# A causal attention kernel: twelve probability buffers, and weighted sums issued five steps behind the scores instead of three

## The chip, the cores and the metric

The program runs on one core of a Trainium2 chip. A core has a matrix engine (TensorE, PE), a vector engine (VectorE, DVE), a scalar engine (ScalarE, ACT), a general engine (GpSimd, POOL), and a queue engine (SyncE, SP) that issues transfers and here computes nothing. Each engine runs its own list of instructions in order and waits on semaphores that others raise. The metric is the device time of one execution in microseconds (us), lower is better.

## The reference

A block with layer norm, then attention and a ternary feed-forward side by side, both added to the input. The change touches the attention alone: 4 batches, 16 heads of 16 dimensions, 2048 positions, causal.

```
xn = layernorm(x)                                   # x: (4, 2048, 256)
q, k, v = heads of xn (two small projections each, rotary part on half of q and k)
scores = (q @ k.T) / sqrt(16);  masked above the diagonal
y = softmax(scores) @ v;  out = x + y @ Wc + ffn(xn)
```

## The kernel before

Three stages follow each other: projections and feed-forward (to about 520 us), attention (to about 1925 us), and the output projection. `attention` works through 16 *quads*, a quad being four heads of one batch. One quad has two kinds of work, and they run at the same time, for different quads.

**Maxima.** For softmax each query row needs its maximum first. `SEQ` lists 139 *entries* for a quad: PE writes a block of scores (128 queries by up to 512 keys) into one of three banks `sm` (L1146), and DVE reduces it to one number a row (L1109; L1094 where the diagonal's mask is added; L1105 where `excess` is added, which stands for a second block: PE forms the difference of two blocks in `st`, L1155 and L1158, and ACT takes its positive part, L1044). Three entries of the list, the *rows*, gather the maxima of a group of queries: DVE reduces them (L1070), PE transposes them (L1142), DVE splits them into two fp16 parts `mh` and `ml` (L1078, L1080), and SP copies these with 16 small transfers into spare rows of `Q` in SBUF (`load_m`, L939). There they act as an additive term of the scores. The groups are the query chunks (0, 1), (2) and (3), a chunk being 512 queries.

**Probabilities.** For a chunk `c` the key blocks `j` are taken in turn, each as a *pair* of *units* of two heads. A quad has 40 pairs: 4 in chunk 0, then 8, 12 and 16. PE computes a unit's scores into one of the two buffers `st` (`scores`, L1170), ACT writes the exponential to one of eight buffers `prob` (L1051), POOL clears the triangle of diagonal blocks (L1009), and PE adds the pair's weighted sums and row sums into the bank `pv` (`weighted_sums`, L1183). Within a chunk the last four pairs are diagonal, 512, 384, 256 and 128 columns wide. After a chunk's last sums ACT copies `pv` to `Y` (`evac`, L1034), and the next chunk's first sums wait for that copy (`pv_read`).

**The order.** PE's order in one quad is the string `TIMETABLE`, a letter for each step: `m` an entry of the maxima (75 entries, `AHEAD`, are always done for the quad before its scores begin, so the string begins with entry 75 of this quad and ends with entry 74 of the next), `x` a difference, `s` a unit of scores, `w` the weighted sums of a pair. ACT follows the same string for `x`, `s` and the copies. `LAG` says with how many pairs of the quad before the string's `w` begin: with 3 the first three `w` are pairs 37 to 39 of the quad before. DVE's order is that of the entries alone.

**SP's order for a quad** (`body` in `@block.sync`) is fixed in the code: wait until all sums of the quad before are done (`pair_used`), load Q and K of the quad after next (12 transfers, L859), load V of the next one (L928), then `load_m` for group 1 and group 2 of this quad and group 0 of the next, then wait for the copy of chunk 3 (`pv_read`), and store `Y` and its row sums (8 transfers, L956 and L957). The copy of chunk 3 stands in the next quad's string, behind that string's `LAG`-th `w`. The first unit of chunk 2 (unit 24) waits on PE until the rows of group 1 have landed (`m_loaded`), the first unit of chunk 3 (unit 48) for those of group 2. In the last quad nothing is loaded, and in the first nothing is stored first.

Of the kernel before, what the change touches and what calls it, by code (L numbers as in the profile page):

```python
# [733 lines left out]

ST, SM, PT = 2, 3, 8
SLOTS = 3
UNITS = sum(2 * G * (c + 1) for c in range(TC))
PAIRS = UNITS // 2  # L740
# [41 lines left out]

AHEAD = 75
XAHEAD = sum(e < AHEAD + LEAD for e in EXCESS)
LAG = 3

ORDER = [(c, j, CH - P * max(0, j - SUB * c)) for c in range(TC) for j in range(SUB * (c + 1))]

# [1 line left out]
def block_width(t, k):  # L790
# [4 lines left out]


TIMETABLE = (
    "ssmmwmmsmswsmmswxmmxmwsmsmmssmwmswsmsmmwxmmsmwmmsmmxmwmmssmmwmmsmsws"
    "mmxmxmmwmmssmmsmsssmmwmsmxmmsmwsmmwxmsmmwsmmmsmswsmmsmwsmsmmwsmmxmms"
    "mmwsmsmmwmsmmswmsmmswsmxmmswmsmsmsmmwsmmmsmwwmmssmmwsmmmswsmmmswsmmm"  # L800
    "swmmssmwsmmmswsmmswsmmmswmsmsmmwsmmsmwmsmsmmwmsmxmmsmwmmsxmmsmwsmsm"
)


def tokens():

    plan, e, x, u, n = [], AHEAD, XAHEAD, 0, -LAG
    for c in TIMETABLE:
# [9 lines left out]
        else:  # L818
            plan.append(("sums", -1 if n < 0 else 0, n % PAIRS))
            n += 1  # L820
    assert (e, x, u, n) == (NE + AHEAD, NX + XAHEAD, 2 * PAIRS, PAIRS - LAG)
    return plan
# [39 lines left out]
def attention(nc, w, scr):  # L862

    with ExitStack() as ctx:
# [52 lines left out]
        def quads(body):  # L917

            for quad in range(NQ):
                body(quad, quad % SLOTS, quad == NQ - 1)  # L920
# [211 lines left out]
        def _(pe):  # L1132
# [41 lines left out]
            def weighted_sums(quad, slot, n, last):  # L1174
                c, j, width = order[n]
                if j == 0:
                    pe.wait_ge(pv_read, quad * TC + c + 1)
                if diag[n]:
                    pe.wait_ge(masked, quad * DIAG + 2 * sum(diag[:n + 1]))
                else:  # L1180
                    pe.wait_ge(exp_done, unit_done(quad, NUMBERS[last][2 * n + 1]))
                for h in range(G):
                    i = pe.matmul(pv[2 * DH * h:2 * DH * (h + 1), CH - width:CH], lhsT=V[slot][:, j, h, :],  # L1183
                                  rhs=prob[(slot * UNITS + 2 * n + h // 2) % PT][:, h % 2, 0:width],
                                  start=j == 0, stop=j == SUB * (c + 1) - 1, tile_position=(0, 2 * DH * h))
                    if h == G - 1:
                        i.then_inc(pair_used, 1)
# [30 lines left out]
            quads(body)  # L1218
            for n in range(PAIRS - LAG, PAIRS):
                weighted_sums(NQ - 1, (NQ - 1) % SLOTS, n, True)  # L1220
# [220 lines left out]
```

## Time and profile before

| | us |
|---|---|
| median of 3 runs (lowest, highest) | 2054.63 (2052.05, 2055.58) |
| the profiled execution | 2050.78 |
| its span | 2049.0 |
| PE busy | 1939.1 (95%) |
| DVE busy | 1795.2 (88%) |
| ACT busy | 1578.8 (77%) |
| POOL busy | 359.0 (18%) |
| attention, steady quads: one quad | 84.4 to 86.6 |

The engines' busy times are those of the profiled execution. PE's times are modelled, so its share is no measure of how near it is to its peak. The granted clock is given as a share of 2.4 GHz, and 0.50 is 1.2 GHz. ACT does nothing in the output projection, which is why its share of the whole is lower than its share of a quad.

### The profile page before, as it was taken

To read this page: it belongs to the slowest core of one execution; us is meant where nothing else is said; L and a number is where in the kernel's file an instruction comes from. 1 tells how busy PE (TensorE), PEld (TensorE's weight loads), DVE (VectorE), ACT (ScalarE), POOL (GpSimd) and SP (SyncE) were. 2 spreads that over 40 slices of the span, in tenths; PEclk is the share of its full clock that TensorE was granted. 3 is DMA by queue.
4 is the path that set the end of the run, shared out by engine and by line. 5 is a ranking of instruction groups with operands and counts; after the bars stand their busy time and mean duration, and the time that the engine had idled before them with its cause. 6 is when DMAs were issued, how large, how long until landed. Compare 5 with 4: busy or idle time off the path is not lost. (4 is left out here: it accounts for less than half of the span.)

```text
span 2049.0 us, 42600 instructions
## 1 busy us (share of the span) xinstructions
PE 1939.1 (95%) x14289; PEld 733.6 (36%) x14289; DVE 1795.2 (88%) x4744; ACT 1578.8 (77%) x2078; POOL 359.0 (18%) x618
## 2 busy tenths in 40 slices
PE   7899999999699999999999999999999999999698
PEld 6455555555222222222222222222222222222165
DVE  5699999999889999999999989999999999997187
ACT  2566666666089999999899989999999999999500
POOL 0112221111112121221212212122121221211000
PEclk8999999999589999999999999999999999999889
DMA  4133333325411230311303113031130321300376
GB/s 165 42 89 94 99 97 102 86 87 126 91 28 23 32 54 2 54 30 26 54 2 54 31 24 54 2 54 32 24 54 2 53 38 18 54 2 13 101 211 206
DMA packets 146213, 123.32 MB, mean 60 GB/s; under 512 B 82068, under 2 KB 132668, under 8 KB 144572
## 3 DMA queue, kind: packets, MB, share of 16 engines
q1 hardware_dynamic: 137324, 112.55, 25.3%
q10 hardware_dynamic: 8720, 8.65, 1.4%
q8 instruction: 89, 1.46, 0.3%
q14 instruction: 80, 0.66, 0.1%
HBM read 69.50 MB, written 50.86 MB: 59 GB/s over the span
## 5 line engine op out<-in xcount | busy, mean ns | idle before, releaser
L1051 ACT ACTIVATE prob<-st 128x1024 f32<-128x1024 f32 (+3 forms) x1280 | 1071.7, 898 | 83.3 <-PE st L1170 75.4
L1183 PE MATMUL pv<-prob,V 128*32 128x512 f32 (+3 forms) x5120 | 598.6, 542 | 0.1
L1146 PE MATMUL sm<-K,Q 48*128 48x512 f16 (+3 forms) x2176 | 542.1, 350 | 17.0 <-DVE pm L1109 4.7
L1094 DVE CUSTOM_DVE_ANT_0 sm<-sm,mask 128x128 f32<-128x128 f32 (+3 forms) x1024 | 490.5, 510 | 61.1 <-PE sm L1146 53.7
L1109 DVE TENSOR_REDUCE pm<-sm 128x1 f32<-128x512 f32 x768 | 494.6, 685 | 15.0 <-PE sm L1146 12.6
L1170 PE MATMUL st<-Q,K 50*128 50x512 f16 (+3 forms) x2560 | 472.5, 353 | 21.5 <-ACT prob L1051 10.9
L1009 POOL TENSOR_SCALAR_AFFINE_SELECT prob<-prob 128x256 f32<-128x256 f32 x512 | 206.1, 409 | 1116.5 <-ACT prob L1051 1111.4
L1146 PEld LDWEIGHTS sm<-K,Q 48*128 48x128 f16 x2176 | 173.8, 94 | 392.6 <-DVE pm L1109 156.6
L1105 DVE CUSTOM_DVE_ANT_0 sm<-sm,excess 128x512 f32<-128x512 f32 x384 | 264.8, 716 | 25.5 <-PE sm L1146 16.2
L1170 PEld LDWEIGHTS st<-Q,K 50*128 50x128 f16 x2560 | 125.3, 93 | 408.5 <-ACT prob L1051 321.7
L1044 ACT ACTIVATE excess<-st 128x1024 f32<-128x1024 f32 x188 | 190.4, 1032 | 5.1 <-DVE pm L1105 0.7
L1183 PEld LDWEIGHTS pv<-prob,V 128*32 128x32 f32 x5120 | 102.5, 108 | 161.0 <-issue 123.7
L1094 DVE DVE_READ_ACCUMULATOR2_ANT pm<- 128x1 f32 x1024 | 144.5, 141 | 0.2
L639 ACT ACTIVATE g<-bank 128x512 f32<-128x512 f32 x128 | 76.7, 599 | 54.7 <-PE bank L708 54.7
L669 PE MATMUL bank<-wWP,gh 128*128 128x256 f16 x512 | 113.7, 273 | 0.0
L669 PE MATMUL bank<-wWP,gl 128*128 128x256 f16 x512 | 113.5, 272 | 0.0
L533 DVE SCALAR_TENSOR_TENSOR gl<-g,wlnw,gh 128x512 f16<-128x512 f32 x128 | 91.9, 758 | 6.5 <-ACT gh L642 6.5
L1296 DVE RECIPROCAL rl<-sums 16x512 f32<-16x512 f32 x16 | 53.3, 3333 | 47.3 <-DMA sums<-scratch_l 47.3
L642 ACT ACTIVATE gh<-g,wlnw 128x512 f16<-128x512 f32 x128 | 93.5, 731 | 0.0
L1155 PE MATMUL st<-K,Q 48*128 48x512 f16 x384 | 81.0, 389 | 9.1 <-ACT prob L1051 7.2
L644 ACT ACTIVATE g<-g 128x512 f32<-128x512 f32 x128 | 81.4, 636 | 0.0
L1158 PE MATMUL st<-NK,Q 48*128 48x512 f16 x384 | 80.7, 384 | 0.0
(151 smaller groups left out, 1896.2 us busy)
## 6 DMA issues: line engine op xcount, KB each, us to landing
Q<-scratch_q SPq DMA_DIRECT2D x102, 128.0 KB, 4.0
K<-scratch_k SPq DMA_DIRECT2D x102, 128.0 KB, 6.2
x<-in_x SPq DMA_DIRECT2D x18, 512.0 KB, 4.5
scratch_v<-Vs SPq DMA_DIRECT2D x64, 128.0 KB, 2.0
scratch_r<-R SPq DMA_DIRECT2D x16, 512.0 KB, 3.2
V_raw<-scratch_v SPq DMA_DIRECT2D x16, 512.0 KB, 8.8
scratch_y<-Y SPq DMA_DIRECT2D x64, 128.0 KB
Yt<-scratch_y SPq DMA_DIRECT2D x16, 512.0 KB, 5.8
```

The source lines that it names most:

```text
L533: dve.scalar_tensor_tensor(out=gl[:, hc, :], in0=g[:, hc, 0, :], scalar=w["lnw"][:, hc:hc + 1], in1=gh[:, hc, :], op0=ALU.mult, op1=ALU.su ...
L642: act.activation(gh[:, hc - 1, :], g[:, hc - 1, 0, :], ACT.Copy, scale=w["lnw"][:, hc - 1:hc])\
L669: pe.matmul(bank[s][:, 0:C], lhsT=x[:, hc, s * P:(s + 1) * P], rhs=w["WP"][:, hc, :], start=hc + k == 0, stop=hc + k == HC)
L1009: pool.affine_select(out=x, in_=x, compare_op=ALU.is_ge, fill=0.0, base=0, pattern=[[0, 2], [1, P]], channel_multiplier=-1).then_inc(maske ...
L1044: act.activation(excess[((slot + ahead) % SLOTS * NX + k) % EXCESSES][:, :, :], st[number % ST][:, :, :], ACT.Relu)\
L1051: act.activation(prob[(slot * UNITS + k) % PT][:, :, 0:width], st[number % ST][:, :, 0:width], ACT.Exp)\
L1094: dve.tensor_tensor_reduce(x, x, mask[:, CH - width:], 1.0, -3e38, ALU.add, ALU.max, pm[:, row, t, k:k + 1]).then_inc(sm_read, 1)
L1105: dve.tensor_tensor_reduce(x, x, excess[(slot * NX + r) % EXCESSES][:, h % 2, :], 1.0, -3e38, ALU.add, ALU.max, pm[:, row, t, k:k + 1]).th ...
L1109: dve.tensor_reduce(out=pm[:, row, t, k:k + 1], in_=x, axis=AX.X, op=ALU.max).then_inc(sm_read, 1)
L1146: pe.matmul(dst[:, 0:block_width(t, k)], lhsT=Q[slot][r, h // 2, t * P:(t + 1) * P], rhs=K[slot][r, h // 2, k * CH:k * CH + block_width(t, ...
L1170: i = pe.matmul(st[number % ST][:, a, 0:width], lhsT=K[slot][r, u % 2, j * P:(j + 1) * P], rhs=Q[slot][r, u % 2, (c + 1) * CH - width:(c + ...
L1183: i = pe.matmul(pv[2 * DH * h:2 * DH * (h + 1), CH - width:CH], lhsT=V[slot][:, j, h, :], rhs=prob[(slot * UNITS + 2 * n + h // 2) % PT][: ...
```

## The change

`PT`, the number of probability buffers, goes from 8 to 12; a score unit can be computed six pairs ahead of its sums instead of four. `LAG` goes from 3 to 5, so that each string's first five `w` belong to the quad before. The string is another order of the same letters. After the last quad five pairs of sums are left to do instead of three.

```
-ST, SM, PT = 2, 3, 8
+ST, SM, PT = 2, 3, 12
...
-LAG = 3
+LAG = 5
...
-    "ssmmwmmsmswsmmswxmmxmwsmsmmssmwmswsmsmmwxmmsmwmmsmmxmwmmssmmwmmsmsws"
...
+    "mxxmmwmsmmswmsmmswsmmswsmmswssmmwsmmmswsmsmwmmsmsmmwxmxmmwmmsmswmsmm"
```

DVE's order is the same. PE and ACT keep their instructions but for the order. These are ACT's rows from the start of a quad's units to its copy of chunk 3 of the quad before. `prob<-st` is a unit's exponential (128x1024 is two heads of 512 columns), `excess<-st` a difference, `Y<-pv` the copy. Before:

```order
L1051 ACTIVATE prob<-st 128x2x256
L1051 ACTIVATE prob<-st 128x2x128 x2
L1051 ACTIVATE prob<-st 128x1024 x2
L1051 ACTIVATE prob<-st 128x2x384 x2
L1051 ACTIVATE prob<-st 128x2x256 x2
L1034 ACTIVATE Y<-pv 128x512
```

And now:

```order
L1051 ACTIVATE prob<-st 128x2x128 x2
L1044 ACTIVATE excess<-st 128x1024 x2
L1051 ACTIVATE prob<-st 128x1024 x2
L1051 ACTIVATE prob<-st 128x2x384 x2
L1051 ACTIVATE prob<-st 128x2x256 x2
L1051 ACTIVATE prob<-st 128x2x128 x2
L1034 ACTIVATE Y<-pv 128x512
```

The 2x128 rows ahead of the others close the quad before. Behind them the copy came after six units; now it comes after two differences and eight units.

These are ACT's rows from behind that copy to the end of chunk 1; the first unit of chunk 2 follows them. Before:

```order
L1044 ACTIVATE excess<-st 128x1024 x2
L1051 ACTIVATE prob<-st 128x2x128 x2
L1051 ACTIVATE prob<-st 128x1024 x5
L1034 ACTIVATE Y<-pv 128x512
L1044 ACTIVATE excess<-st 128x1024
L1051 ACTIVATE prob<-st 128x1024 x2
L1044 ACTIVATE excess<-st 128x1024
L1051 ACTIVATE prob<-st 128x1024 x3
L1051 ACTIVATE prob<-st 128x2x384 x2
L1044 ACTIVATE excess<-st 128x1024 x2
L1051 ACTIVATE prob<-st 128x2x256 x2
L1051 ACTIVATE prob<-st 128x2x128 x2
```

And now:

```order
L1051 ACTIVATE prob<-st 128x1024 x8
L1034 ACTIVATE Y<-pv 128x512
L1044 ACTIVATE excess<-st 128x1024 x2
L1051 ACTIVATE prob<-st 128x1024 x2
L1051 ACTIVATE prob<-st 128x2x384 x2
L1044 ACTIVATE excess<-st 128x1024 x2
L1051 ACTIVATE prob<-st 128x2x256 x2
L1051 ACTIVATE prob<-st 128x2x128 x2
```

Two differences and two units of 128 columns have gone from between the copy and chunk 2. Counted in the two strings, with all letters:

| stretch of the string | letters before | letters now |
|---|---|---|
| start to the last `w` of the quad before | 7 m, 6 s, 0 x, 3 w | 13 m, 8 s, 2 x, 5 w |
| from there to unit 24 (chunk 2) | 36 m, 18 s, 6 x, 9 w | 29 m, 16 s, 4 x, 7 w |
| the rows entry of group 2 to unit 48 (chunk 3) | 17 m, 10 s, 1 x, 5 w | 14 m, 9 s, 0 x, 4 w |
| fewest units between a pair's own and its sums | 2 | 6 |

## Rows read from the trace of the kernel before

**Rows 1.** Busy time in one quad: us, each engine, granted clock, DMA share, GB/s.

```profile
827.15:911.68 84.53, 82.52 (x671) 23.02 (x668) 78.36 (x235) 79.34 (x97) 16.60 (x35) 1.00 0.21 33
```

**Rows 2.** Waits of the whole run: who waited for whom, us, times, longest.

```profile
PEld pv L1183 <- POOL prob L1009: 13.0, 53, 0.5
...
PEld pv L1183 <- ACT Y L1034: 6.6, 33, 0.4
...
PEld st L1170 <- DMA Q<-ml: 6.4, 12, 1.3
```

**Rows 3.** Timeline of SP in a steady quad: start, duration, instruction, count.

```profile
827.77 0.35 SPq L956 DMA_DIRECT2D scratch_y<-Y  x1
...
830.86 3.48 SPq L859 DMA_DIRECT2D Q<-scratch_q  x6
...
837.66 7.39 SPq L939 DMA_DIRECT2D Q<-mh  x4
845.10 2.42 SPq L939 DMA_DIRECT2D Q<-ml  x4
```

**Rows 4.** Timeline of ACT: the copy of chunk 3 in six quads.

```profile
827.15 0.59 ACT L1034 ACTIVATE Y<-pv 128x512 f32<-128x512 f32 x1
...
911.68 0.59 ACT L1034 ACTIVATE Y<-pv 128x512 f32<-128x512 f32 x1
...
996.34 0.60 ACT L1034 ACTIVATE Y<-pv 128x512 f32<-128x512 f32 x1
...
1082.49 0.60 ACT L1034 ACTIVATE Y<-pv 128x512 f32<-128x512 f32 x1
...
1166.85 0.60 ACT L1034 ACTIVATE Y<-pv 128x512 f32<-128x512 f32 x1
...
1253.45 0.60 ACT L1034 ACTIVATE Y<-pv 128x512 f32<-128x512 f32 x1
```

**Rows 5.** Timeline of PE's weight loads: chunk 2 begins, wait for the rows.

```profile
848.72 0.12 PEld L1170 LDWEIGHTS st<-Q,K 50*128 50x128 f16 x2 [0.28 <-DMA Q<-ml]
...
933.27 0.10 PEld L1170 LDWEIGHTS st<-Q,K 50*128 50x128 f16 x2 [0.30 <-DMA Q<-ml]
...
1018.41 0.11 PEld L1170 LDWEIGHTS st<-Q,K 50*128 50x128 f16 x4 [0.79 <-DMA Q<-ml]
...
1104.06 0.12 PEld L1170 LDWEIGHTS st<-Q,K 50*128 50x128 f16 x2 [0.28 <-DMA Q<-ml]
...
1189.45 0.11 PEld L1170 LDWEIGHTS st<-Q,K 50*128 50x128 f16 x4 [1.33 <-DMA Q<-ml]
```

**Rows 6.** ACT's waits from the copy to chunk 2 of one quad.

```profile
ACT prob L1051 <- PE st L1170: 1.4, 4, 0.5
```

**Rows 7.** Timeline of ACT: units back to back, 512 and 128 columns wide.

```profile
829.62 0.66 ACT L1051 ACTIVATE prob<-st 128x256 f32<-128x256 f32 x2
...
879.36 7.65 ACT L1051 ACTIVATE prob<-st 128x1024 f32<-128x1024 f32 x8
```

**Rows 8.** Timeline of PE: one pair's sums, and what follows them.

```profile
879.70 1.06 PE L1183 MATMUL pv<-prob,V 128*32 128x512 f32 x8
880.70 0.39 PE L1170 MATMUL st<-Q,K 50*128 50x512 f16 x2
```

**Rows 9.** Busy time and granted clock behind two longer waits, as in rows 1.

```profile
1020.00:1022.00 2.00, 2.00 (x16) 0.78 (x10) 1.25 (x6) 1.17 (x2) 0.00 (x0) 0.50 0.00 0
1190.00:1193.00 3.00, 3.00 (x18) 0.81 (x16) 1.51 (x4) 1.89 (x2) 0.00 (x0) 0.50 0.00 0
```

**Rows 10.** Timeline of all engines: from group 2's transposition to unit 48.

```profile
864.68 0.33 PE L1142 MATMUL sm<-ident,m 128*128 128x128 f32 x1
...
868.19 2.47 SPq L939 DMA_DIRECT2D Q<-ml  x4
...
874.67 0.39 PE L1170 MATMUL st<-Q,K 50*128 50x512 f16 x2
```

**Rows 11.** Timeline of PE: the last three pairs of sums of attention.

```profile
1920.62 1.76 PE L1183 MATMUL pv<-prob,V 128*32 128x384 f32 x24
```

More of the change, by code:

```diff
@@ L797 @@
 TIMETABLE = (
-    "ssmmwmmsmswsmmswxmmxmwsmsmmssmwmswsmsmmwxmmsmwmmsmmxmwmmssmmwmmsmsws"
-    "mmxmxmmwmmssmmsmsssmmwmsmxmmsmwsmmwxmsmmwsmmmsmswsmmsmwsmsmmwsmmxmms"
-    "mmwsmsmmwmsmmswmsmmswsmxmmswmsmsmsmmwsmmmsmwwmmssmmwsmmmswsmmmswsmmm"
-    "swmmssmwsmmmswsmmswsmmmswmsmsmmwsmmsmwmsmsmmwmsmxmmsmwmmsxmmsmwsmsm"
+    "mxxmmwmsmmswmsmmswsmmswsmmswssmmwsmmmswsmsmwmmsmsmmwxmxmmwmmsmswmsmm"
+    "smxmxmmwmmssmsmssmsmmwsmsmmwsmmxmwsmmxmwwmmssmwmmsmswsmmmswmssmmwmms"
+    "msmmwsmmmswmmsmswmmssmwsmmssmswmmsmsmmwsmmsmmwwsmmsmwmmsmxmmsmwmsmms"
+    "wmsmmswmmsmswmmsmswmsmswmmsmsmmxmmsmwmsmmswsmmmsmxmmswmsmmxsmmwmsms"
 )
```

## The prediction

> **What bounds the kernel now.** I first read the busy time of the engines in one steady quad, taken from one copy of chunk 3 to the next [rows 1]. In 84.53 us PE is busy for 82.52, ACT for 79.34 and DVE for 78.36, and the clock is full. No engine has more than some 6 us to spare, and with two buffers `st` and three banks `sm` between them none can run far ahead. So 5 or 6 us of a quad are lost in handing over, and whatever stops PE for longer than these few buffers last stops all three.
>
> Next the list of waits [rows 2], for what the change can take away. The sums' weight loads wait for POOL's triangle for 13.0 us in the whole run, 53 times, and for the copy of `pv` for 6.6 us. The same list has a third wait, a small one: scores wait 6.4 us for the transfer of `ml`, 12 times. It is small in sum, but an engine that waits twelve times for a little is one whose supplier is only just in time. So I followed that supplier back in the timelines.
>
> SP's timeline of one quad [rows 3] starts at 827.77, right behind ACT's copy of chunk 3, which began at 827.15 [rows 4]. It stores Y until 830.86, issues the Q, K and V loads, then comes to the rows of group 1 at 837.66. Four tiny transfers of `mh` take it 7.39 us there, which I read as a queue full of the 2 MB before them, and the four of `ml` are out at 845.10 + 2.42 = 847.52. PE's first unit of chunk 2 goes at 848.72, after waiting 0.28 us for them [rows 5], so landing takes 1.2 us. From the copy to that release it is 848.72 - 827.15 = 21.57 us. The four other quads shown [rows 4, 5] have 21.59, 22.07, 21.57 and 22.60; the mean is 21.9. Without the wait PE would have been there after 21.57 - 0.28 = 21.29 us, and in the others after 21.29, 21.28, 21.29 and 21.27. So two chains of nearly equal length start at the copy: SP's, 21.6 to 22.6 us, and the order's, 21.3 us. SP's chain wins by 0.3 to 1.3.
>
> **The change part by part.** *The copy moves, unit 24 does not.* The later `w` put the copy of chunk 3 behind 13 entries and 8 units instead of 7 and 6, while unit 24 stays at the same place in the string (letter 84, from 85). SP's list is unchanged and hangs on that copy, so its chain keeps its 21.9 us, but starts later. The order's chain from the copy to unit 24 becomes shorter, and each engine gives a figure for how much:
>
> - DVE: 29 entries instead of 36. The 36 went by in 21.3 us, 0.59 each, so seven fewer are 4.1 us: 17.2 us are left.
> - PE: two pairs of sums fewer at 880.70 - 879.70 = 1.0 us each [rows 8], 2.0 us from these alone, and also seven entries, two differences and two narrow units. That goes with DVE's figure.
> - ACT: two differences at 7.65 / 8 = 0.96 us, and two narrow units at 0.66 / 2 = 0.33 [rows 7], 2.6 us: 18.7 are left if ACT's idle 1.4 us in this stretch [rows 6] stay. Without them it would be 17.3.
>
> ACT now has the most to do in the stretch, so its figure counts, with most of its idle time: I take 18.2 us, between 17.2 and 18.7. PE then stands at unit 24 for 21.9 - 18.2 = 3.7 us in each quad, from 2.9 (21.6 - 18.7) to 4.7 (21.9 - 17.2). What is queued behind that unit is everything on PE: entries for DVE, units for ACT, sums. ACT has at most two narrow units of 0.33 us left, DVE at most three entries of 0.6, so neither bridges it, and nothing later returns the time, since the next copy and SP's next list come late by the same amount. The wait occurs in the strings of quads 1 to 14: quad 0 has no copy in front, and in quad 15 there are no loads to queue behind. Today these 14 quads wait 6.4 us in all, 0.46 each. Added: 14 x (3.7 - 0.46) = 45 us (bounds 34 and 59).
>
> *The clock.* Two of the five waits shown are longer than 0.7 us (0.79 and 1.33), and behind each the granted clock falls to 0.50, that is from 2.4 to 1.2 GHz [rows 9]. Behind the 0.3 us waits it stays. What this costs is to be seen in the time from the release to the next copy [rows 4, 5]: 62.96, 63.07 and 62.79 us where the clock stayed, 64.08 and 64.00 where it fell, 1.1 us more. With 3.7 us of standing PE it should fall in all 14 quads, twelve more than in these rows: 12 x 1.1 = 13 us (bounds 0 and 21, if a longer stop costs as much as 1.5).
>
> The Trainium skill, page "TensorE: Matmul & The Clock Gate", section "HAM oscillation — how this bites in real kernels", says that a kernel whose matmuls wait for a transfer in every tile drops to the lower clock in every tile, and that this costs half of the throttled time. Applied to the 3 us at 0.50 of the second row of rows 9 this is 1.5 us a quad instead of the 1.1 that the copies show, and the sum would be 5 us higher. I use the 1.1, since it is this kernel's own.
>
> *Twelve buffers, five steps.* A pair's sums now come at least 6 units after its own instead of 2, so the waits for POOL's triangle should go (13.0 us) and those for the copy may shrink (6.6 us) [rows 2]. They lie on PE, but ACT and DVE often have work queued over 0.3 us. The gain is between 0 and 19.6 us. I take 8, nearer to the lower half, because the waits left are all of the short kind that the buffers cover in part, and because the string has the same letters and the same total work for each engine. ACT's wait for a free `prob` keeps its margin of one pair (6 - 5 as 4 - 3).
>
> *The new order in itself* has the differences nearer to the entries that use them: the shortest lead falls from 5 entries to 2. DVE may wait for ACT there. This is inside the 0 of the gain's lower bound, for DVE has 6 us to spare a quad [rows 1].
>
> *The tail.* Five pairs instead of three are left after the last unit. Two of 512 columns are added to the 1.76 us that three take [rows 11], 2.0 us; some of it runs under ACT's last units. I take +1.7.
>
> Sum: +45 + 13 - 8 + 1.7 = +52 us. Against the profiled execution, 2050.8 + 52 = 2102.8 us. The median of the runs before is 3.9 us above that execution; I add about half of this, 2105 us.
>
> **The rivals.**
>
> *The stop is there, the clock holds or recovers for nothing* (2091 us). The clock term disappears and a little of the stall, 52 - 13 = 39 on top, plus 1. For it: the chip granted full clock behind most of the short waits. Against: both longer waits shown lost it.
>
> *A second gate opens, at unit 48* (2117 us). The chain from group 2's transposition to landed rows is 868.19 + 2.47 + 1.2 - 864.68 = 7.2 us, and unit 48 comes after 10.0 us [rows 10]. In the new string this stretch has one pair of sums (1.0 us), one difference, one unit and three entries less, about 2.2 us in all by like steps, so 7.8 us are left. 0.6 us of slack can vanish. A wait of 0.8 us in 15 quads is 12 us more. For it: the slack is of the size of the spread between quads. Against: it is still positive, and SP is idle by then.
>
> *Faster* (2044 us). The order's chain from the copy to unit 24 does not shorten to less than SP's, because PE, which must still do its later sums, is slower in this stretch than I think, or because SP's chain becomes shorter than 21.6 us when it starts later and nothing else moves data. Then only the gain and the tail are left: -8 + 1.7 = -6 us, and with the whole 19.6 even -18 (2033). It decides if the distance from the copy to unit 24 stays at or above 21.5 us. Against: this needs three engines with 3 to 5 us less work in the stretch to take as long as now; for it: I can't see in this trace whether the 7.39 us of `mh` is a fixed time or would shrink.
>
> *The change does nothing that counts* (2050 us). A wait of 0.5 us more in each quad, eaten by the gain.
>
> **How the numbers follow.** The forecast has a chance of 0.50, the stop without the clock's loss 0.20, the second gate 0.15, faster 0.11, no change 0.04. Slower is thus 0.85. A measurement of this kernel can tell 0.2% (4 us) from no change. The range takes in the bounds of the terms: the low end has 34 + 0 - 10 + 1 = +25, about 2077, and the high end 59 + 21 + 0 + 2 = +82, 2133 at the outermost, of which I keep 2129. Outside are the faster cases and the far corners.
>
> **What would show it.** Right: PE's weight loads of L1170 wait for the transfer of `ml` some 50 us in total, 14 times and 3 to 5 us each, about 21.9 us after each copy of chunk 3; the clock reads 0.50 for some us behind each; a quad takes 88 to 89.5 us instead of 85.1; the time from release to the next copy grows from 63 to about 67; pv's waits for POOL are gone; ACT and DVE idle with PE named. Wrong: quads of 84 us, no row with more than 1.5 us on `ml`, or SP's `mh` issues shorter than 5 us. If the wait is there and the quad still takes less than 87 us, then the new order has won more than my 8 us.

## The result, and the profile after

The changed kernel takes 2132.6 us (median of 4 runs, 2131.17 to 2133.83) against 2055.1 us, a ratio of 1.0373, interval 1.0349 to 1.0398. It is slower, as forecast, but by 77.5 us and not by 50, and 2132.6 lies above the range that ended at 2129.

Two steady quads of the changed kernel, from copy to copy, and stretches behind the stops of these quads (columns as in rows 1: us, busy time of PE, PEld, DVE, ACT, POOL with counts, granted clock, DMA share, GB/s):

```profile
750.58:840.02 89.44, 83.89 (x669) 22.89 (x667) 78.13 (x234) 79.62 (x96) 16.59 (x35) 0.98 0.19 31
840.02:931.69 91.67, 85.00 (x669) 23.06 (x667) 78.40 (x234) 79.73 (x98) 16.61 (x35) 0.96 0.19 31
772.00:775.00 3.00, 3.00 (x15) 0.48 (x13) 1.82 (x4) 1.94 (x2) 0.00 (x0) 0.50 0.00 0
775.50:778.50 3.00, 2.95 (x26) 0.77 (x26) 2.77 (x8) 2.98 (x4) 0.00 (x0) 1.00 0.01 3
862.00:866.00 4.00, 3.94 (x17) 0.76 (x19) 1.82 (x4) 1.94 (x2) 0.00 (x0) 0.50 0.00 0
864.00:867.00 3.00, 3.00 (x15) 0.43 (x7) 1.24 (x4) 1.36 (x2) 0.00 (x0) 0.50 0.00 0
```

Against [rows 1] DVE and ACT are busy for the same time, but the quad is 5 to 7 us longer: the time went into standing. The clock reads 0.50 behind each stop, and while it does DVE and ACT are busy for only about half of the time (1.82 and 1.94 us of the 4 from 862.00 on). It does not stay there equally long: behind the first stop it is full again from 775.50, behind the second it is still low at 867.00. Over the 14 quads with a stop, six have the clock low for 3.4 us and eight for 6.8 us, and all stops of 4 us and more are among the eight.

The waits of the whole run, those that answer to [rows 2]:

```profile
ACT prob L1051 <- PE st L1170: 134.9, 201, 4.9
...
PEld st L1170 <- DMA Q<-ml: 55.4, 14, 4.8
...
PEld pv L1183 <- ACT Y L1034: 18.9, 62, 0.4
...
PEld pv L1183 <- POOL prob L1009: 6.4, 19, 0.4
```

The wait for `ml` was 6.4 us in 12 times and is now 55.4 us in 14, just the 14 quads that were counted. The sums' wait for POOL's triangle fell from 13.0 to 6.4 us, but the wait for the copy rose from 6.6 to 18.9.

SP's list in the same quad as [rows 3]:

```profile
840.65 0.35 SPq L956 DMA_DIRECT2D scratch_y<-Y  x1
...
843.74 4.46 SPq L859 DMA_DIRECT2D Q<-scratch_q  x6
...
851.75 6.76 SPq L939 DMA_DIRECT2D Q<-mh  x4
858.55 2.42 SPq L939 DMA_DIRECT2D Q<-ml  x4
```

ACT's copy of chunk 3 in two quads, and how ACT goes on around the second one's stop:

```profile
750.58 0.60 ACT L1034 ACTIVATE Y<-pv 128x512 f32<-128x512 f32 x1
...
840.02 0.60 ACT L1034 ACTIVATE Y<-pv 128x512 f32<-128x512 f32 x1
...
856.24 1.80 ACT L1051 ACTIVATE prob<-st 128x512 f32<-128x512 f32 x4 [0.31 <-PE st L1170]
862.78 1.94 ACT L1051 ACTIVATE prob<-st 128x1024 f32<-128x1024 f32 x2 [4.74 <-PE st L1170]
```

And PE's weight loads where these quads begin chunk 2, which answer to [rows 5]:

```profile
771.53 0.10 PEld L1170 LDWEIGHTS st<-Q,K 50*128 50x128 f16 x2 [3.51 <-DMA Q<-ml]
...
862.06 0.10 PEld L1170 LDWEIGHTS st<-Q,K 50*128 50x128 f16 x2 [4.59 <-DMA Q<-ml]
```

*Arrival* is here the point at which PE would have gone on without the wait. From copy to release it is 20.95 and 22.04 us, from copy to PE's arrival 20.95 - 3.51 = 17.44 and 22.04 - 4.59 = 17.45. So SP's chain kept its length within its spread (21.4 us on average over the 14 quads, against 21.9 in the rows of before) and the order's fell from 21.3 to 17.45. After the release PE needs 840.02 - 771.53 = 68.5 us and 931.69 - 862.06 = 69.6 us to the next copy.

### The profile page after: what moved, and what is told of

It reads as the page before. It is cut to its first block and busy times, and to the rows that moved or that the text cites. A ratio compares the mean times of both kernels' runs of the same rounds, so it can differ in the third digit from the quotient of the medians.

```text
span 2129.4 us, 42602 instructions
## 1 busy us (share of the span) xinstructions
PE 1965.8 (92%) x14289; PEld 733.0 (34%) x14289; DVE 1793.7 (84%) x4744; ACT 1583.6 (74%) x2078; POOL 359.0 (17%) x618
## 5 line engine op out<-in xcount | busy, mean ns | idle before, releaser
L1183 PE MATMUL pv<-prob,V 128*32 128x512 f32 (+3 forms) x5120 | 607.4, 552 | 0.1
L1170 PE MATMUL st<-Q,K 50*128 50x512 f16 (+3 forms) x2560 | 498.5, 360 | 74.3 <-DMA Q<-ml 53.5
L1146 PE MATMUL sm<-K,Q 48*128 48x512 f16 (+3 forms) x2176 | 548.2, 358 | 16.4 <-DVE pm L1109 4.2
L1109 DVE TENSOR_REDUCE pm<-sm 128x1 f32<-128x512 f32 x768 | 489.6, 684 | 68.3 <-PE sm L1146 63.7
L1105 DVE CUSTOM_DVE_ANT_0 sm<-sm,excess 128x512 f32<-128x512 f32 x384 | 264.2, 722 | 19.6 <-PE sm L1146 17.1
L1155 PE MATMUL st<-K,Q 48*128 48x512 f16 x384 | 77.5, 386 | 11.2 <-ACT prob L1051 7.1
L708 PE MATMUL bank<-xh,wWF 128*128 128x512 f16 x256 | 78.1, 387 | 1.5 <-DVE xl L527 1.5
```

Of the source, the lines that this page charges most:

```text
L1105: dve.tensor_tensor_reduce(x, x, excess[(slot * NX + r) % EXCESSES][:, h % 2, :], 1.0, -3e38, ALU.add, ALU.max, pm[:, row, t, k:k + 1]).th ...
L1109: dve.tensor_reduce(out=pm[:, row, t, k:k + 1], in_=x, axis=AX.X, op=ALU.max).then_inc(sm_read, 1)
L1146: pe.matmul(dst[:, 0:block_width(t, k)], lhsT=Q[slot][r, h // 2, t * P:(t + 1) * P], rhs=K[slot][r, h // 2, k * CH:k * CH + block_width(t, ...
L1170: i = pe.matmul(st[number % ST][:, a, 0:width], lhsT=K[slot][r, u % 2, j * P:(j + 1) * P], rhs=Q[slot][r, u % 2, (c + 1) * CH - width:(c + ...
```

## The experiments

All ratios are against the kernel before on the same chip. Its median was 2054.0 us beside the first four, 2050.9 beside the next three and 2053.2 beside the last two.

**Rows first in SP's list, in both orders.** The edit, the same in both kernels, for E1 (before) and E2 (changed):

```
             def body(quad, slot, last):
+                load_m(quad, slot, 1)
                 if not last:
                     sp.wait_ge(pair_used, quad * PAIRS + PT // 2)
...
                     load_v(quad + 1)
-                load_m(quad, slot, 1)
                 load_m(quad, slot, 2, last)
```

> The kernel before, but SP sends the rows of group 1 ahead of the Q, K and V loads of its list; nothing else is changed. Theory (SP's list behind the copy of chunk 3 sets when unit 24 may start): the waits for ml (6.4 us) and the two falls of the clock (2 x 1.1) go, so 6 to 9 us less, about 2046. Rival (the new order itself is what costs): the same figure for this kernel, but see the next run. Rival 2 (the loads are needed early, so that sending them later starves the next quads): slower than before.

> The changed kernel with the same edit of SP's list. Theory A (the stop at unit 24, the clock behind it and the restart are the whole loss): all of the 78 us come back, 2045 to 2058, quads of 84 to 84.6 us. Theory B (a part of the loss lies in the new order itself, about 1 to 2 us in each quad, since quads grew by 5.5 us and the waits by only 3.5 and the clock by 1.1): 2065 to 2080, quads of 85.5 to 86.5 us, with no wait for ml.

E1: 2045.84 us, 0.9962 (0.9947 to 0.9977), as expected. E2: 2054.52 us, 1.0004 (0.9985 to 1.0023), within theory A's 2045 to 2058. SP's list in E2:

```profile
835.12 0.28 SPq L957 DMA_DIRECT2D scratch_l<-Y  x1
837.33 2.45 SPq L939 DMA_DIRECT2D Q<-mh  x4
839.82 2.42 SPq L939 DMA_DIRECT2D Q<-ml  x4
842.28 2.77 SPq L859 DMA_DIRECT2D Q<-scratch_q  x6
```

The four transfers of `mh` take 2.45 us where only the stores of `Y` stand ahead of them. Two quads of E2 and one of E1:

```profile
746.91:831.71 84.80, 82.49 (x669) 22.66 (x667) 78.43 (x234) 79.69 (x98) 16.60 (x35) 1.00 0.23 33
831.71:916.77 85.06, 82.71 (x669) 22.67 (x667) 78.43 (x234) 79.69 (x96) 16.59 (x35) 1.00 0.22 33
```

```profile
827.23:911.77 84.54, 82.53 (x671) 23.03 (x668) 78.38 (x235) 79.37 (x98) 16.62 (x35) 1.00 0.24 33
```

With this edit alone the changed kernel gives back all of its 78 us: no wait for `ml` is left, and the clock stays in all steady quads but one (it reads 0.50 for some us at 1275, and that quad takes 86.6 us). So the stop and what it draws after it are the loss; theory A holds for the size. But E2 is not as fast as E1. With the gate out of the way in both, the changed kernel (order, lag and buffers together) is 2054.5 - 2045.8 = 8.7 us slower, 85.06 us against 84.61 a quad on average; 1.5 us of the 8.7 are the longer tail, and some 0.1 of the 0.45 a quad are the one fall of the clock. Theory B was right that the order costs something, but it is a quarter to a half of the 1 to 2 us that it said.

**The lag without the string (E3), the string without the lag (E4).** E3 is the kernel before with `PT = 12` and `LAG = 5`, E4 the changed one with `PT = 8` and `LAG = 3`:

```
-ST, SM, PT = 2, 3, 8          # E3; in E4 12 becomes 8
+ST, SM, PT = 2, 3, 12
-LAG = 3                       # E3; in E4 5 becomes 3
+LAG = 5
```

> The string of before with 12 buffers and sums five pairs behind: the same letters in the same places, every w stands for a pair two earlier, and the copy of chunk 3 comes at the fifth w (letter 30) instead of the third (letter 15). Theory: from the copy to unit 24 there are now some 16.4 us (7 entries, four units and two differences less), SP's chain takes 21.3, so 4.9 us of wait in 14 quads, plus the clock: 2125 to 2140. Rival (the new string is what costs, not the lag): within 10 us of the kernel before.

> The new string with 8 buffers and sums three pairs behind; the copy of chunk 3 then comes at its third w (letter 17). From there to unit 24 there are 34 entries and four more units: about 20 us, so 1.3 us of wait in 14 quads instead of 4. Theory: 2085 to 2100. Rival (the new string itself costs 1 to 2 us a quad beside the waits): at the upper end of this or above, up to 2115; rival (the string is what costs all): near 2130.

E3: 2194.4 us, 1.0668 (1.0632 to 1.0703), far above its 2125 to 2140. E4: 2104.3 us, 1.0246 (1.0216 to 1.0275), above the theory's 2085 to 2100 and inside the rival's, which went up to 2115. In E3 PE waits at unit 24 in 11 of the 14 quads, 3.8 us on average. Where the clock was full on the way there it arrives after 17.0 us, close to the 16.4 expected; in the other three quads the clock was low for 17 us from the copy on, and PE came too late to wait. In E4 it arrives after 21.14 us, not after 20, and waits 3.5 us in all, 8 times. One such row of each, E3's and then E4's:

```profile
974.75 0.13 PEld L1170 LDWEIGHTS st<-Q,K 50*128 50x128 f16 x4 [4.60 <-DMA Q<-ml]
```

```profile
856.65 0.10 PEld L1170 LDWEIGHTS st<-Q,K 50*128 50x128 f16 x2 [0.58 <-DMA Q<-ml]
```

The lag makes the stop without the new string (and E7 below shows no such stop with the buffers alone), so the theory holds for where it comes from. Both kernels also lose outside the stop. E4's quads take 87.9 us on average, 3.3 more than E1's 84.6, with 0.25 us of wait in them. E3's take 94.4, 9.8 more than E1's, and the waits are 3.0 of these; how the rest divides between the clock, which is low for 10 us a quad there, and the order is not separated. A string is fitted to one lag. With another lag each `w` is the sums of another pair, wide where it was narrow. The list of waits fits this, though no run isolates it: in E3 ACT waits 181 us for scores and the sums 35 us for the copy.

```profile
ACT prob L1051 <- PE st L1170: 181.1, 305, 5.1
...
PEld pv L1183 <- ACT Y L1034: 35.3, 51, 1.3
```

I had left this out of both expectations. It also means that neither the lag nor the string does well without the other.

**PE kept busy in the stop (E5, E8).** Sixteen matmuls ahead of the wait, in quads 1 to 14, into the buffer that unit 24 overwrites. In E5 they use 48 rows of the array, in E8 all 128 (`lhsT=ones[:, 0:P], rhs=ones[:, :]`):

```
+                if u == 24 and 0 < quad < NQ - 1:
+                    for _ in range(FILLER):       # FILLER = 16
+                        pe.matmul(st[number % ST][:, 0, :], lhsT=K[slot][0:KD, 0, 0:P],
+                                  rhs=Q[slot][0:KD, 0, 0:CH], start=True, stop=True)
+                    pe.wait_ge(m_loaded, ...)     # the wait of before, moved behind them
```

> The changed kernel with 16 matmuls of 512 columns, about 3.5 us, put on PE ahead of the wait for the rows at unit 24 of quads 1 to 14; they write into the buffer that the unit then overwrites. The stop stays as long as it is (about 21.4 us from the copy), but PE is not idle in it. Theory (the stop costs its length, and what a quad pays beyond it is the clock at 1.2 GHz behind the stop): the time from the release to the next copy falls from 69.2 to about 67.5 us, and the kernel from 2132 to 2106 to 2112. Rival (what is paid beyond the stop is the restart with empty buffers, not the clock): the clock stays at 1.00 and the time stays within 6 us of 2132.

> As the kernel that put 16 matmuls ahead of the wait at unit 24, but each of them now uses all 128 rows and 128 columns of the array instead of 48 rows. With the 48-row matmuls the clock held in 4 of 14 quads, and these quads took 88.15 us against 89.2 to 92.9 in the others. Theory (what a quad pays beyond the length of the stop is the clock alone): if the clock holds now in all 14, each takes 88.1 to 88.7 us and the kernel 2095 to 2102. Rival (the clock does not depend on this filling): it falls as before, and the time stays at 2130.

E5: 2131.7 us, 1.0389 (1.0352 to 1.0426), nothing gained. The rival's time came true and its condition did not: in 10 of 14 quads the clock fell as in the changed kernel, in 7 of them while the 16 matmuls still ran. In three of these the fall came early, the 16 took 5.9 us instead of 3.6, and unit 24 went only 22.8 to 23.0 us after the copy, so E5 also lengthened some of its stops. In the 4 quads where the clock held, a quad took 88.14 to 88.43 us, in the others 90.6 to 92.9. One stop of E5, and what follows it:

```profile
765.50:769.50 4.00, 4.00 (x19) 1.74 (x21) 0.65 (x3) 0.35 (x1) 0.89 (x3) 0.88 0.07 12
769.50:775.50 6.00, 6.00 (x30) 1.20 (x26) 3.35 (x9) 3.84 (x4) 0.00 (x0) 0.51 0.00 0
```

E8: 2106.9 us, 1.0271 (1.0248 to 1.0294). The same stretch:

```profile
767.50:771.50 4.00, 3.91 (x21) 1.67 (x22) 1.04 (x4) 0.69 (x3) 1.20 (x4) 1.00 0.02 4
771.50:775.50 4.00, 3.99 (x32) 0.84 (x34) 3.26 (x9) 3.59 (x4) 0.00 (x0) 1.00 0.00 0
```

PE's busy time is full or nearly so in both, yet the clock holds only in E8, and there in every steady quad. The quads take 88.3 to 89.5 us, and from release to copy PE needs 67.1 to 67.6 us, where E2 has 67.3 (a quad of 84.8 less 17.45). So with the clock kept a stop costs its length and nothing more: (2106.9 - 2054.5) / 14 = 3.7 us a quad, for stops that last 4.0 us in the changed kernel. The clock costs the rest, (2132.6 - 2106.9) / 14 = 1.8 us. Restarting with empty buffers is not visible. The time came out 5 us above the expected 2095 to 2102, because I had taken only the best quads of E5 for it.

**The load of V behind the rows (E6).** In the changed kernel:

```
-                    sp.wait_ge(v_placed, quad + 1)
-                    load_v(quad + 1)
                 load_m(quad, slot, 1)
+                if not last:
+                    sp.wait_ge(v_placed, quad + 1)
+                    load_v(quad + 1)
```

> The changed kernel with the load of V (512 KB) behind the rows of group 1 in SP's list instead of ahead of them; Q and K (1.5 MB) stay ahead. Theory (the rows wait in a queue for the data ahead of them, so the chain shrinks with these bytes): a quarter of about 14 us, 3.5 us less, a chain of about 18 us and a wait of 0.5 us, clock mostly kept: 2065 to 2078. Rival (the 6 to 7 us at the mh transfers are a fixed cost of that form of transfer or of the switch to it): the chain shrinks only by the 0.4 us of the issue, and the time stays at 2120 or above.

E6: 2060.5 us, 1.0037 (1.0021 to 1.0054).

```profile
750.48 4.35 SPq L859 DMA_DIRECT2D Q<-scratch_q  x6
754.88 2.75 SPq L859 DMA_DIRECT2D K<-scratch_k  x6
757.68 2.44 SPq L939 DMA_DIRECT2D Q<-mh  x4
760.16 2.42 SPq L939 DMA_DIRECT2D Q<-ml  x4
```

The mh transfers take 2.44 us, so the 6 to 7 us were no fixed cost of theirs. In the quads where PE still waits, the chain is 17.7 to 19.4 us instead of 21.4, and the waits are 0.25 to 1.7 us, 9.4 in all. This agrees with a queue that is full of the data ahead. It does not show that the bytes count: E6 moves the one transfer of 512 KB, and whether its size or its own form held up the `mh` transfers is not separated. The time was even below the 2065 to 2078 expected; the clock fell in two quads only.

**Twelve buffers alone (E7).** The kernel before with `PT = 12`.

> The kernel before with 12 probability buffers and nothing else. All theories: no part of the loss lies in the buffers. ACT nearly never waits for a free one today, so within 4 us of the kernel before. Rival (the larger buffers change where the other tensors lie and disturb some engine): more than 6 us slower.

2052.6 us, 1.001 (0.9987 to 1.0033). No effect of the buffers is seen; the interval leaves room for 3 us of gain or 7 of loss.

**The sums behind each copy two letters later (E9).** E2's kernel, four places of the string; one of them:

```
-    "...mswsmsmwmmsmsmmwxmxmmwmmsmswmsmm"
+    "...mswsmsmwmmsmsmmwxmxmmmmwsmswmsmm"
```

> The changed kernel with the rows first in SP's list, and in its string the first w behind each of the four copies moved two letters later. In that kernel this w waits 0.2 to 0.4 us for the copy, 62 times, 19.3 us in all, against 6.6 us in the order of before. Theory (these waits are why the new order is 0.45 us a quad slower once the stop is gone): the waits fall under 8 us and 4 to 8 us come back, about 2048. Rival (PE has time to spare there, the order loses elsewhere, or the moved letters starve another engine): no gain or a loss, 2053 or more.

2099.5 us, 1.0235 (1.0212 to 1.0258), 45 us slower than E2. The waits of E2 and of E9:

```profile
ACT prob L1051 <- PE st L1170: 57.1, 193, 1.6
...
PEld pv L1183 <- ACT Y L1034: 19.3, 62, 0.4
```

```profile
ACT prob L1051 <- PE st L1170: 101.0, 267, 2.0
```

The wait for the copy is down to 0.4 us, once, as intended, and ACT's wait for scores has grown by 44 us, about the size of the loss. So the waits for the copy are not shown to be why the new order is 8.7 us slower; taking them away in this way costs much more. What makes those 0.45 us a quad stays open.

## Why the prediction was wrong in size and right in kind

The four differences between kernels add up to the whole: after - E8 is the clock, E8 - E2 the stop, E2 - E1 the new order, and E1 - before takes off what the gate cost already. The medians were taken beside different runs of the kernel before, whose own medians differ by 2 us (2053.2 beside E8, 2054.0 beside E1 and E2, 2055.1 beside the changed kernel), so the first two differences are no finer than that.

| term | forecast | measured |
|---|---|---|
| stop at unit 24, over the 6.4 us of before | +45 | 52.4, less 6.4: +46 |
| clock behind it, over the two falls of before | +13 | 25.7, less about 2: +24 |
| new order and lag | -8 | +8.7 with the tail |
| tail | +1.7 | in the line above |
| sum | +52 | +78.7 |

The sum missed by 27 us. The stop was right to 1 us. Two terms failed: the clock gave 11 us too little, and the term for the new order, with the tail, 15 us too little. The bounds of the terms reached 2133, and I kept only 2129; the result lay in the 4 us between them. That it lay below 2133 at all was luck, since the clock and the order were both beyond their bounds, and the stop, well inside its own, made up for them.

*What bounds the kernel, and the two chains.* Right. The supplier of a wait of 6.4 us in all was the one that decided. E1 also shows that it cost the kernel before 8.1 us, its waits and its clock.

*The copy moves, unit 24 does not.* Right: 14 waits, 55.4 us, 3.96 each against 3.7 forecast. PE arrives after 17.45 us, not 18.2. This is DVE's figure of 17.2 rather than ACT's 18.7: of ACT's 1.4 us of idle time in the stretch 0.3 were left, where I had kept most of it. SP's chain was half a microsecond shorter than its mean of before, which took back some of that. The two misses hid each other in the 3.96.

*The clock.* The mechanism was right, all 14 quads lost it, and the size was wrong: 1.8 us a quad, not 1.1. The step that failed is the price of one fall. I took it from two quads in which the clock was low for 3.4 us, and counted one such fall in each quad. That price holds where the fall is as short: the six quads of the changed kernel with 3.4 us need 68.5 to 68.7 us from release to copy, 1.2 to 1.4 more than E2's 67.3. In the other eight the clock is low for 6.8 us, and they need 69.0 to 70.2 us, 1.7 to 2.9 more. My bound of 1.5 us for a longer stop was too low for this.

The condition was also looser than I wrote. I showed two waits above 0.7 us in the kernel before and a fall behind both, but its trace has a third, of 1.31 us, with none:

```profile
1276.13 0.11 PEld L1170 LDWEIGHTS st<-Q,K 50*128 50x128 f16 x4 [1.31 <-DMA Q<-ml]
...
1276.13:1278.13 2.00, 2.00 (x18) 0.53 (x18) 1.50 (x4) 1.51 (x2) 0.02 (x1) 1.00 0.01 4
```

So a wait of that length may or may not bring a fall; behind the 14 stops of 3.1 to 4.8 us it always came. Nor does the length of a wait set alone how long the clock stays low: in E7 it was low for 10.2, 6.8 and 3.4 us behind waits of 1.05, 0.97 and 0.70 us. And in E2 it fell once with no wait for a transfer at all, at 1275 us, where PE had been busy for 3.05 of the 3.5 us before, in the narrow units that stand ahead of chunk 2:

```profile
1271.50:1275.00 3.50, 3.05 (x27) 0.91 (x19) 3.17 (x11) 2.94 (x6) 1.54 (x4) 1.00 1.05 142
1275.10:1278.30 3.20, 3.20 (x15) 0.63 (x15) 1.50 (x5) 1.68 (x3) 0.00 (x0) 0.50 0.99 136
```

What decides it in the short cases stays open.

The rule of the Trainium skill, page "TensorE: Matmul & The Clock Gate", section "HAM oscillation — how this bites in real kernels", that half of the throttled time is lost, gave 1.5 and would have been nearer. The traces bear out its first half, that the clock falls in every round in which PE waits for a transfer, only for the long waits: in all 14 quads of the changed kernel, but behind 2 of the 12 short waits of the kernel before. Of the second they show somewhat less than half: in the changed kernel the clock is low for 66 us behind the releases, and these stretches from release to copy take 26 us more than 14 times E2's 67.3.

*Twelve buffers, five steps.* This is the step that failed in sign. I allowed 0 to 19.6 us of gain and no loss, because the letters and the work were the same. E2 against E1 gives +8.7, some 7 without the tail. The waits for POOL fell only by half (13.0 to 6.4), and the waits for the copy, which "may shrink", tripled (6.6 to 18.9). E4 and E9 show how much an order can cost with the same letters: 3 us a quad for a lag that the string was not made for, 45 us for four `w` moved by two letters. So "the same work" was no bound at all. Where the 7 us of the changed order are lost stays open; E9 shows only that its waits for the copy cannot be removed in that way. With 0 in the place of the -8 the forecast would have been 2113, and with a bound on both sides the range would have held the result.

*The rivals.* The stop without the clock's loss did not happen, though E8 shows what it would have been, 2107 and not 2091. The second gate did not open. In the quad shown the transposition for group 2 is at 880.87, `ml` is out at 884.35 + 2.47, and unit 48 goes at 889.23:

```profile
880.87 0.33 PE L1142 MATMUL sm<-ident,m 128*128 128x128 f32 x1
...
884.35 2.47 SPq L939 DMA_DIRECT2D Q<-ml  x4
```

```profile
889.23 0.39 PE L1170 MATMUL st<-Q,K 50*128 50x512 f16 x2 [0.17 <-ACT prob L1051]
```

That leaves 1.2 us after landing by the 1.2 us of before, more than the 0.6 that I gave it. *Faster* failed at its stated point: PE stood at unit 24 after 17.45 us and not after 21.5. Its open question is answered too: the 7.39 us of `mh` were no fixed time, they shrink to 2.45 in E2.

*The tail* was about right. Five pairs close attention in 3.22 us, where [rows 11] had 1.76 for three:

```profile
1998.31 3.22 PE L1183 MATMUL pv<-prob,V 128*32 128x512 f32 x40
```

That is 1.5 us more, for 1.7.

The fastest version found is E1, the kernel before with the rows sent first: 2045.8 us, 0.4% below it. Buffers and lag play no part in it.

## What to carry to other kernels

A wait that is short but occurs in every round deserves a walk back along its supplier: if that supplier's list starts at an event which a change moves, the wait grows by nearly the whole shift (here by 3.5 us of 3.85). Send the few bytes that an engine will need next ahead of megabytes that are needed a round later. And in an order fitted by hand or by search, no part can be moved at no price: bound it on both sides, however equal the work.

## What the runs showed of the hardware

- With 16 filling matmuls ahead of the wait the clock fell in 10 of 14 stops when they used 48 rows of the array (E5), in 7 of these while they ran back to back, and in none when they used all 128 rows (E8). Why the one filling holds it and the other does not is not settled; they differ also in their data (Q and K in E5, a constant in E8).
- Four 1 KB transfers took SP 5.7 to 8.3 us to issue behind the loads of Q, K and V, 2 MB in 13 transfers (quads 1 to 14 of the two kernels), and 2.4 to 2.8 us behind the loads of Q and K alone, 1.5 MB in 12, or with no load ahead (E6, E2; the stores of `Y` stand ahead in all of them). Whether the bytes, the number of transfers or the form of V's own make the difference is not shown.
- A stop of 4 us in PE's own work cost about its length and nothing for the restart, if the clock is held: 3.7 us a quad (E8 against E2).
- Behind the stops of the changed kernel the clock stayed at 0.50 for 3.4 or 6.8 us, which cost 1.2 to 1.4 and 1.7 to 2.9 us a quad. It fell once without any stop (E2), and a wait of 1.31 us left it full (the kernel before).
